# Taking 22 pipeline drains out of VectorE's queue in an eight-core recurrent-attention-MoE layer

## The reference

```
x  = LN(x_in)
xp = silu(x W_in);  a = sigmoid(xp W_alpha + b);  bv = sigmoid(xp W_beta + b) * tanh(xp W_v + b)
h_t = a_t * h_(t-1) + bv_t;     x1 = x_in + (h * silu(h)) W_out
y  = LN(x1);  r = rmsnorm(y)
q = r Wq;  k, v = split((r Wdown) Wup)          # 16 heads of 64
att = softmax(q k^T / 8) over the 16 heads of one token;   u = y + (att v) Wo
h2 = rmsnorm(u);  gate = softmax(h2 Wg)
out = x1 + u + sum_e gate_e * (h2 We_e)
```

## Time and profile before

| | us |
|---|---|
| median of 2 runs | 4120.55 (4023.89 and 4217.20) |
| the profiled execution, its own time | 4040.64 |
| its span on the slowest core (core 6) | 4038.5 |
| spans of the eight cores | 4002.1 to 4038.5 |
| mean granted PE clock of the cores | 0.755 to 0.758 |

### The profile page before, as it was taken

One profiled execution on the slowest core, in us unless ns is written; L12 is line 12 of the kernel. 1 busy time (PEld: TensorE's weight loads), 2 busy tenths in 40 slices (PEclk: granted clock), 3 DMA queues, 4 the chain that ended last, 5 costly groups with the idle time before them and its releaser, 6 DMA issues.

```text
span 4038.5 us, 38166 instructions; the slowest of 8 cores (4002.1 to 4038.5 us)
## 1 busy us (share of the span) xinstructions
PE 2550.6 (63%) x12352; PEld 1189.6 (29%) x12352; DVE 1561.8 (39%) x2201; ACT 875.7 (22%) x1642; POOL 79.9 (2%) x143
## 2 busy tenths in 40 slices
PE   3555766547774487644975459663596536965378
PEld 1222322223332233222432224331243222432234
DVE  1353323443334433344324533246432463234532
ACT  2322003311123201332023220242103411023110
POOL 0000000000000000000000000000000000000000
PEclk8766878757886688866888569885697857977579
DMA  8631672202321023300222003220032200512013
GB/s 169 137 77 42 120 192 70 77 1 75 134 105 42 22 73 115 125 22 22 104 104 105 21 22 125 104 84 21 21 146 84 105 1 25 163 63 84 1 49 118
DMA packets 44475, 319.87 MB, mean 79 GB/s; under 512 B 5048, under 2 KB 5304, under 8 KB 28928
## 3 DMA queue, kind: packets, MB, share of 16 engines
q0 software_dynamic: 35040, 283.53, 22.8%
q1 hardware_dynamic: 9248, 33.91, 2.2%
HBM read 301.07 MB, written 48.23 MB: 86 GB/s over the span
## 4 chain that ended last, share of the span: by engine, by line
PE 50%; DVE 17%; DMA 9%; DVEq 9%; issue 7%; ACT 7%; ACTq 1%; SPq 0%; POOLq 0%; POOL 0%
PE bank L1430 20%; PE bank L605 3%; PE bank L1137 3%; DMA w<-we 3%; PE bank L831 3%; DMA w<-wscr 3%; PE bank L431 3%; PE bank L1371 3%; PE bank L478 2%; DVEq L920 2%; DVE sstat L1024 2%; DVE kpot L923 2%; DVEq L1023 2%; DVEq L1104 2%; PE bank L958 2%
## 5 line engine op out<-in xcount | busy, mean ns | idle before, releaser
L1430 PE MATMUL bank<-qpg,w 128*128 128x512 bf16 x4096 | 915.1, 387 | 83.4 <-DVE qpg L1403 44.0
L1430 PEld LDWEIGHTS bank<-qpg,w 128*128 128x128 bf16 x4096 | 406.6, 100 | 600.5 <-issue 137.3
L1403 DVE TENSOR_TENSOR qpg<-xph,ybuf 128x4096 bf16<-128x4096 bf16 x64 | 283.2, 4425 | 505.3 <-PE bank L1430 503.8
L1057 PE MATMUL bank<-cpb_s,xph 128*128 128x128 bf16 x512 | 74.8, 300 | 362.5 <-DVE xph L1034 359.3
L1009 ACT ACTIVATE hfm<-bank,sstat 128x128 bf16<-128x128 f32 x512 | 146.0, 368 | 719.2 <-DVE sstat L984 706.9
L1447 ACT ACTIVATE acomb<-bank 128x512 f32<-128x512 f32 x64 | 38.2, 597 | 1139.9 <-PE bank L1430 1136.1
L514 PE MATMUL bank<-xph,w 128*128 128x512 bf16 x512 | 134.3, 409 | 132.2 <-DMA w<-wscr 64.3
L605 PE MATMUL bank<-ln1g,w 128*128 128x512 bf16 x512 | 128.5, 418 | 96.3 <-DMA w<-wscr 73.8
L984 DVE TENSOR_REDUCE sstat<-bank 128x4 f32<-128x512 f32 x128 | 88.5, 691 | 240.6 <-PE bank L970 203.2
L907 PE MATMUL bank<-zb,wupb 64*128 64x512 bf16 x128 | 73.2, 584 | 162.9 <-DVE vpu L923 118.9
L923 DVE TENSOR_SCALAR kpot<-bank,cph_s 64x512 bf16<-64x512 f32 x128 | 95.1, 743 | 201.1 <-PE bank L907 189.7
(11 more groups left out here) (139 smaller groups left out, 3045.3 us busy)
## 6 DMA issues: line engine op xcount, KB each, us to landing
w<-wscr POOLq DMA_DIRECT2D x105, 2048.0 KB, 8.1
wscr<-w POOLq DMA_DIRECT2D x15, 2048.0 KB, 8.9
w<-we POOLq DMA_DIRECT2D x8, 2048.0 KB, 20.4
out<-tmstage SPq DMA_DIRECT2D x16, 1024.0 KB, 4.0
slotA<-x SPq DMA_DIRECT2D x4, 2048.0 KB
slotB<-x SPq DMA_DIRECT2D x4, 2048.0 KB, 11.9
w<-w_inT POOLq DMA_DIRECT2D x1, 2048.0 KB, 28.5
w<-w_aT POOLq DMA_DIRECT2D x1, 2048.0 KB, 22.9
```

The costliest lines, as they stand in the source:

```text
L1403: r = v.tensor_tensor(qpg[:, (e % 2) * 4096:(e % 2) * 4096 + 4096] .rearrange("p (c q) -> p c q", q=512), h2v[:, :, :], ybuf[:, e * 512:(e ...
L1430: last_pe = pe.matmul(bk[:, :], wslice(wbuf, kc, mc), qpg[:, (e % 2) * 4096 + kc * 512: (e % 2) * 4096 + (kc + 1) * 512], start=(e == 0 an ...
```

## The change

Twenty-two `v.drain()` are taken out, each the one that stands at a function's start behind its waits. All waits, all semaphore increments, all DVE operations and their order stay, on every engine. The drains between dependent operations inside a function stay too, and so do those of the small statistics functions whose inputs DVE itself had just written. In one tile the 22 places give 174 drains (1 each at lines 239, 681, 1294, 1324, 1353, 1459; 8 each at 410, 455, 543, 575, 646, 807, 1182, 1248, 1385, 1402, 1493; 16 each at 920, 983, 1023, 1071, 1104), 1392 in the program.

```diff
@@ -235,8 +235,6 @@
                 if t > 0:
                     v.wait_ge(s_se.h, tok[("ln2r", t - 1)])
-                if True:
-                    v.drain()
                 r = v.tensor_reduce(
...
```

## The result

The changed kernel takes 0.9722 of the time of the kernel before, with a 95% interval of 0.9693 to 0.975: 2.8% less. Its median is 3922.8 us over 11 runs; its profiled execution took 3923.3 us with a span of 3921.3, 117 us less than the profiled execution of before. A second set of runs on another chip gave 0.9739 (0.9685 to 0.9792). Some executions of every kernel here have four cores that share a die at a lower PE clock and take longer; the ratios leave them out.

A forecast was written before the change was run, and what follows sets the result against it. No engine is full; engines wait for one another, and drains count in attention, k/v and beta/v. 8.7 + 1.25 + 1.15 + 1.55 = 12.65 us a tile, 100 us in all: 4040.6 to 3940 us, range 3905 to 3960.

The forecast's parts named there:

- Behind work in hand -0.08 in place of +0.09: Where DVE still has work, the next operation starts 0.08 us before the last ends; 0.17 to 0.18 us gained per drain.
- Idle 0.05: Where DVE waits for another engine, removing a drain saves its passage as an instruction, 0.05 us each.
- Attention, 8.7 forecast: Attention: each of sixteen steps loses 0.57 us, 9.1 us, less 0.4 for the ends: 8.7 us a tile.
- Cover at L1087: Attention, PE's product with v: PE would be free 0.28 us before its release, so the whole gain goes through.
- k/v, 1.20 forecast: k/v stage: 15 times 0.08 us, and 0.05 at the first drain, 1.25 us a tile.
- beta/v, 1.15 forecast: beta/v stage: 0.22 us a chunk over five rounds and a bit, 1.15 us a tile.
- The rest: Remaining places, mostly idle cases: add stages 0.75, last chunks 0.25, and 0.2 and 0.35 elsewhere; 1.55 us a tile.
- DVEq to 2% of the chain: DVE's sequencer standing in drains should fall from 9% of the chain that ended last to about 2%.
- held everywhere: Rival, chance 0.09: only L984 to L993 overlaps, each busy drain gives 0.08 us; 63 us in all, 3978 us.
- The engine does it anyway: Rival, chance 0.07: DVE empties itself after each operation, so only idle places gain; 20 us in all, 4021 us.
- PE closes the round: Rival, chance 0.05: no cover at PE's product with v, so 0.34 us an attention step is lost; 3984 us.
- The clock of PE falls in beta/v: Rival, chance 0.03: PE stays at 1.2 GHz throughout beta/v, costing 20.6 us a tile; 4115 us, 1.8% slower.

The follow-up runs named there:

- met_wait: Kernel before with a long-met wait in place of each of the 22 drains; ratio to the kernel before 0.9854 (0.9792 to 0.9916).
- two_drains: Kernel before with two drains in each of the 22 places; ratio to the kernel before 1.0104 (1.0055 to 1.0154).
- kv_turn: Changed kernel with the k and v copies of odd k/v chunks in the other order; ratio to the kernel before 0.9747 (0.9683 to 0.981).
- rest_only: Kernel before without the 18 drains outside the attention, whose four places keep theirs; ratio to the kernel before 0.9911 (0.9881 to 0.9941).
- att_only: Kernel before without the drains of the four attention places only; 3956.8 us, 0.981 of the kernel before, one run of six.
- waits_dve: Changed kernel with two waits of the attention moved within DVE's queue; ratio to the kernel before 0.9714 (0.9653 to 0.9774).
- best: Changed kernel with odd k/v chunks turned round, two DVE waits moved and PE's three waits reordered; ratio to the kernel before 0.9586 (0.9521 to 0.9651).

## Why the prediction was right

The sign, the mechanism and most of the size came out: 100 us forecast against 112 by the ratio (0.0278 x 4040.6; 101 to 124 by its ends) and 117 between the two profiled executions. A tile (t from 1 to 6) lost 14.2 us where 12.65 were forecast. The terms of attention, k/v and beta/v, which carry the mechanism, came within 0.6, 0.3 and 0.1 us of what was measured; most of what was missing lies in the last term, the rest.

- *Behind work in hand -0.08 in place of +0.09.* Shown in all groups of the attention and at L580 to L544. It is not so everywhere: copies behind PE's transposes came to 0.00 (L411) and -0.06 (L808), and why was not looked into. The choice of the pair L984 to L993 as the row to go by was right. met_wait shows that it is the stand that costs, two_drains that a drain has no fixed price of 0.17.
- *Idle 0.05.* Shown: 0.12 to 0.07 at L576, and DVE's wait before L984 from 2.08 to 2.03 in the median.
- *Attention, 8.7 forecast, 9.3 measured.* One small error. The step lost 0.61 in place of 0.57, in the main since an operation that starts inside the one before is itself recorded some 0.01 shorter (0.69 to 0.68, 0.42 to 0.41). Sixteen times 0.61 is 9.8, of which 9.3 came, so the 0.4 taken off for the ends was about right: the first two steps lost nothing, the next two 0.25 each. The 5.96 us that I read was not the typical step, whose median was 5.87; the difference was right, the level not.
- *Cover at L1087.* Held. The copy ends at 1760.70, PE's transposes at 1760.87, the product starts at 1761.06: 0.19 of pause are left of the 0.28 forecast. The row that I had read was untypical here: from the copy's end to the product it has 0.46, the median is 0.36 before and after. The pause went only when PE's waits were put in order.
- *k/v, 1.20 forecast for the 15 borders (1.25 with its first drain), 0.94 measured.* The one term that came out too large: across a chunk's border +0.03 stands now, not the +0.015 of the pair inside a chunk. 15 x 0.063 is 0.94. It is not the way from the upper half to the lower: kv_turn has v then k inside its odd chunks, at +0.015 too. At a border there is also a wait between the two copies, and the bank changes. A second wait there (met_wait) leaves +0.03; which of the two costs the 0.017 is open.
- *beta/v, 1.15 forecast, 1.12 measured;* the round 4.50 forecast, 4.49 in the median.
- *The rest, 1.55 forecast, 2.8 measured.* The step that failed most. From the end of PE's last product to the start of the last add the three add stages lost 0.42, 0.41 and 0.20, 1.03 in place of 0.75: in the first two every second add is behind work in hand, and I had priced the pairs by the idle case alone. For the same reason the eight L1249 gave 0.36, where 0.05 was booked for the last of them. Another 0.64 us went between the first W_in product on DVE (L456) and the first beta/v product (L544), of which drains explain 0.05; that stretch got 0.34 shorter in rest_only and 0.10 longer in att_only, whose edit does not touch it. It contains a load and a fall and a rise of the PE clock, and I leave it open.
- *DVEq to 2% of the chain.* It is 4%. The drains that stay (L1015 and L546 now) take over as places where the chain sees the sequencer stand, with DVE at work behind them.

Of the rivals, *held everywhere* falls to the attention's gaps, and kv_turn confines it to copies whose input starts in the other half of the partitions. *The engine does it anyway* falls to the same gaps. The Trainium skill's sentence behind it (VectorE: DVE Perf Modes, section The DRAIN you can't avoid), that a semaphore between two operations costs nothing, rests there on eight copies behind one another, and met_wait agrees where DVE has work. Where DVE is idle a further wait cost 0.07 us. *PE closes the round* did not happen with the change. *The clock of PE falls in beta/v* did not happen either: it rose, from 0.92 to 0.94.

## What to carry to other kernels

In this kernel a drain behind a wait costs DVE 0.05 us where it is idle and 0.17 to 0.18 where it has work in hand, because it also forbids the next operation to start 0.08 before the last one ends (0.06 where that operation is held anyway). Waits that are met already are free behind work in hand and cost 0.07 behind the wait that ends last. So in a round that closes over two engines, take out the drains that guard nothing (those in front of an operation that reads nothing the engine itself has just written), and put the wait that is met last at the end: here the first gave 9.3 us of a tile's attention and the second, with two waits moved on DVE and one on PE, another 4.7. The share of a sequencer on the chain is no forecast of the gain: 9% of the chain stood for 2.8% of the time.

## What the runs showed of the hardware that was not expected

The time at which PE's clock rises after the attention is not the same in kernels whose attention and W_o have the same PE instructions. From the last output copy to the rise to 2.4 GHz it took 3.4 us in the median before, 3.7 after, but 5.6 in att_only and met_wait, 5.8 in two_drains, 5.3 in kv_turn, 5.4 in waits_dve and 4.5 in rest_only, and 3.6 in best. These are medians over the tiles and cores of one profiled execution each; a second one of the changed kernel, on another chip, gives 3.7 again, but inside the kernel before single places go from 2.9 to 6.3. What sets it was not tried. W_o is longer where it comes late: from the start of the last output copy to the first add it is 18.5 us in the kernels before and after, 19.2 to 19.3 in att_only, met_wait, two_drains, kv_turn and waits_dve, 18.9 in rest_only, 18.6 in best. Over eight tiles 0.7 to 0.9 us are 6 to 7 us, nearly half of the 14 that kv_turn gained in k/v. An edit worth 10 us in this kernel can be paid back in good part by a stage that it does not touch, and only stretches of the trace tell the two apart.
